# Three more pairs of tiles in reduced-precision parts, and their low parts divided between VectorE and GpSimd

## The chip, the core and the metric

The kernel runs on one core of a Trainium2 chip. The metric is the device time of one execution in microseconds, taken as a median of several executions. The trace of the kernel before is one profiled execution; its times are counted from the start of its span.

## The reference, cut to what matters

For 2048 samples, 39 embedding rows of 16 numbers are looked up. They run through three layers of a compressed interaction network, and a small dense network follows:

```python
x0 = xk = e                                  # [2048, 39, 16]
for idx, (W, b) in enumerate(params):        # three layers, 128 maps each
    z = einsum('bhd,bkd,hks->bsd', x0, xk, W) + b
    z = relu(z)
    # layers 0 and 1: first 64 maps are the next xk, the other 64 go to direct; layer 2: all 128
logit = sum(concat(direct), axis=-1)         # over the 16 numbers: [2048, 256]
h = relu(concat([logit, dense_ctx]) @ W_top1 + b_top1)
h = relu(h @ W_top2 + b_top2);  y = h @ W_top3
```

So each layer multiplies x0 by xk elementwise, for every pair of fields (VectorE), and contracts the products with weights (TensorE). All is float32.

## The kernel before, in words

**Tiling.** The samples are cut into 16 groups of 128, a group into 4 chunks of 32 samples; a chunk has 32 x 16 = 512 columns, 64 chunks in all. The rows (h, k) of a layer are cut into tiles of 128 rows. Layer 0 has 7 tiles of up to 117 rows (symmetric pairs of fields are folded, `x0_diag`), layers 1 and 2 have 20 tiles each, the last of them with only 64 different rows (`x0_pairs`). VectorE makes the products of up to four tiles in one instruction, called a slot here: 2 slots for layer 0, 5 for layer 1, 5 for layer 2. The products go to `prod`, a ring of four slots; a slot is given back when TensorE has finished with it (`slot_free`), so VectorE is at most four slots ahead.

**Plain and split tiles.** A plain tile is one float32 matmul, which the trace shows as two records of TensorE (L686). A split tile is three matmuls (L709) in the type float32r: ScalarE rounds the product to a high part (`pair_hi`, L526), another engine subtracts that from the product and writes the low part (`pair_lo`, `low_part`, L210), and TensorE multiplies high by low weights, low by high weights, and high by high weights. Two tiles are split together, a pair. Before, 11 pairs are split per chunk: 5 in layer 1, 5 in layer 2, 1 in layer 0. The tile of 64 rows is also split, with two matmuls (the half tile, `half_parts`, L522 and L206). The list `SPLITS` gives, for each layer, slot, first tile in the slot and number of tiles. `pair_hi` and `pair_lo` hold two pairs each, so ScalarE may round a pair only when TensorE has finished the pair two before it.

**Who does what.** VectorE makes all products (L412), the low parts of layers 0 and 1, and the sums over the 16 numbers (`sum01` L442, `sum2` L449). GpSimd makes the low parts of layer 2 and, behind them in each chunk, issues that chunk's share of the indirect DMAs that gather the embedding rows of a later group (L345, 39 per group). ScalarE rounds (L526, L522), and applies bias and relu: `hand_on` (L535, L536) makes the next layer's xk in two halves, L562 and L616 make the `direct` parts, L569 does layer 2. It copies x0 to `xk0` in PSUM for the products of layer 0 (L559).

**Order.** Each engine has a written order inside a loop over the groups. TensorE runs, per chunk, layer 1, then layer 0 of the next chunk, then layer 2; in the second chunk of a group it also transposes the next group's embeddings, between layers 1 and 0. VectorE makes the products in the same order, each low part one product behind the product it belongs to. ScalarE runs roundings in order of use; those of layer 2 are interrupted after the fourth entry of its list (`EARLY`) by `hand_on(0, ...)` and `direct_0()`. Products of layer 2 need `xk2`, which needs all of layer 1 from TensorE; products of layer 1 need `xk1` from layer 0, which was made a phase earlier. SyncE and the queue of ScalarE load `x0_pairs` (two buffers) and `x0_diag` for the next chunk.

**End.** After the last chunk the dense network runs on TensorE from `logit01` and `logit2`, which hold the sums of all samples in SBUF (L768).

## Time and profile before

| | us |
|---|---|
| median of 3 executions | 2551.4 (2550.67 to 2551.43) |
| the profiled execution | 2557.0 |
| its span, first to last instruction | 2555.3 |
| TensorE busy with matmuls | 2434.8 |
| VectorE busy | 2269.2 |
| GpSimd busy | 1558.9 |
| ScalarE busy | 1175.5 |

The mean granted TensorE clock is 0.995 of full speed. Matmuls are pipelined and their ends are modelled, so the distance from one start to the next tells what one costs, not the duration of a record. A duration of VectorE, ScalarE or GpSimd is that of the instruction; two instructions behind each other on VectorE overlap by about 0.08 us.

### The profile page before, as it was taken

Reading aid. Unit: us, or ns where it says so; the run is one execution under the profiler, and the core shown is the slowest. Engines: PE = TensorE matmul, PEld = TensorE weight load, DVE = VectorE, ACT = ScalarE, POOL = GpSimd, SP = SyncE. Lnnn points to the kernel's source line nnn. Section 1 sums busy time; section 2 is a strip of 40 time slices with the busy share of each in tenths; the row PEclk is TensorE's granted clock in tenths of the full one; section 3 lists DMA queues with packets and bytes.
Section 4 is the critical chain, followed back from the end, with each engine's and each line's share of the span. In section 5 each row is a group of like instructions: output and inputs, shape, how many; then the busy total and the mean of one; then the engine's idle time right before and its main releaser. Section 6 shows DMA issues by size and latency. Waiting matters only on the chain.

```text
span 2555.3 us, 25999 instructions
## 1 busy us (share of the span) xinstructions
PE 2434.8 (95%) x7712; PEld 1425.0 (56%) x7712; DVE 2269.2 (89%) x1356; ACT 1175.5 (46%) x1414; POOL 1558.9 (61%) x1030
## 2 busy tenths in 40 slices
PE   0499999999999999999999999999999999999999
PEld 0255555555555555555555565555555555555553
DVE  0499999999999999999999999999999999999960
ACT  0145444444444454544444444544444444445442
POOL 6466676666667666766666676667666666743240
PEclk9899999999999999999999999999999999999999
DMA  2977776877678687767867776777778677776610
GB/s 60 231 189 195 204 211 173 218 199 195 183 209 218 179 203 201 210 175 208 212 190 188 215 214 177 199 208 208 175 216 205 186 193 211 209 176 201 195 30 0
DMA packets 262599, 477.02 MB, mean 187 GB/s; under 512 B 19371, under 2 KB 37675, under 8 KB 262501
## 3 DMA queue, kind: packets, MB, share of 16 engines
q1 hardware_dynamic: 141622, 271.05, 39.4%
q10 hardware_dynamic: 100480, 200.29, 28.8%
q0 software_dynamic: 20480, 5.47, 1.4%
q8 instruction: 9, 0.15, 0.0%
q14 instruction: 8, 0.07, 0.0%
HBM read 468.99 MB, written 7.74 MB: 187 GB/s over the span
## 4 chain that ended last, share of the span: by engine, by line
PE 69%; POOL 11%; DVE 6%; issue 5%; DMA 5%; ACT 2%; another core or an unknown queue 1%; SPq 0%; POOLq 0%; DVEq 0%; ACTq 0%
PE z L686 35%; PE z L709 31%; POOL emb L345 6%; DVE prod L412 4%; POOL pair_lo L210 4%; DMA emb<-in_tbl,idx 4%; PE xk L768 1%; PE z L768 1%; ACT pair_hi L526 1%; POOL half_parts L206 1%; DVE logit L442 1%; DVE pair_lo L210 1%; PE turned L667 1%; DMA x_diag<-x_transposed 1%
## 5 line engine op out<-in xcount | busy, mean ns | idle before, releaser
L412 DVE TENSOR_TENSOR prod<-x_pairs,xk 128x2048 f32<-128x2048 f32 x640 | 1436.7, 2284 | 74.7 <-PE z L709 49.6
L686 PE MATMUL z<-prod,w_plain 128*128 128x512 f32 (+2 forms) x2944 | 1383.3, 594 | 41.8 <-issue 26.4
L526 ACT CAST pair_hi<-prod 128x1024 fp32r<-128x1024 f32 x703 | 735.6, 1046 | 1077.5 <-PE z L709 756.0
L210 POOL TENSOR_TENSOR pair_lo<-prod,pair_hi 128x1024 fp32r<-128x1024 f32 x320 | 764.0, 2387 | 641.9 <-ACT pair_hi L526 625.2
L686 PEld LDWEIGHTS z<-prod,w_plain 128*128 128x128 f32 (+2 forms) x2944 | 555.7, 189 | 475.5 <-issue 400.7
L345 POOL DMA_INDIRECT emb<-in_tbl,idx x624 | 701.5, 1124 | 189.4 <-issue 173.2
L709 PE MATMUL z<-pair_hi,w_lo 128*128 128x512 f32 (+1 forms) x1408 | 787.6, 559 | 2.3 <-DVE pair_lo L210 1.7
L709 PE MATMUL z<-pair_hi,w_hi 128*128 128x512 f32 (+1 forms) x1408 | 556.3, 395 | 0.0
L709 PE MATMUL z<-pair_lo,w_hi 128*128 128x512 f32 (+1 forms) x1408 | 555.5, 395 | 0.0
L210 DVE TENSOR_TENSOR pair_lo<-prod,pair_hi 128x1024 fp32r<-128x1024 f32 (+1 forms) x384 | 468.5, 1220 | 49.4 <-ACT pair_hi L526 49.4
L709 PEld LDWEIGHTS z<-pair_hi,w_lo 128*128 128x128 f32 (+1 forms) x1408 | 265.5, 189 | 297.3 <-POOL pair_lo L210 137.1
L709 PEld LDWEIGHTS z<-pair_lo,w_hi 128*128 128x128 f32 (+1 forms) x1408 | 266.3, 189 | 154.7 <-issue 122.9
L412 DVE TENSOR_TENSOR prod<-x_diag,xk 117x2048 f32<-117x2048 f32 (+1 forms) x128 | 257.7, 2014 | 71.4 <-ACT xk L559 71.4
L709 PEld LDWEIGHTS z<-pair_hi,w_hi 128*128 128x128 f32 (+1 forms) x1408 | 264.7, 188 | 65.0
L535 ACT ACTIVATE xk<-z,columns 64x512 f32<-64x512 f32 x128 | 83.0, 648 | 148.6 <-PE z L709 132.1
L206 POOL TENSOR_TENSOR half_parts<-prod,half_parts 64x512 fp32r<-64x512 f32 x64 | 83.2, 1300 | 5.5
L667 PE MATMUL turned<-ident,emb 128*78 128x128 f32 x128 | 18.3, 288 | 69.9 <-DMA emb<-in_tbl,idx 69.9
L536 ACT ACTIVATE xk<-z,columns 64x512 f32<-64x512 f32 x128 | 83.5, 652 | 1.6
L522 ACT CAST half_parts<-prod 128x512 fp32r<-128x512 f32 x128 | 78.7, 615 | 0.0
L442 DVE TENSOR_REDUCE logit<-direct 128x512 f32 (+1 forms) x64 | 67.9, 1060 | 0.0
L335 POOL DMA_DIRECT2D idx<-in_ids x16 | 9.5, 597 | 82.9 <-DMA emb<-in_tbl,idx 82.6
L667 PEld LDWEIGHTS turned<-ident,emb 128*78 128x78 f32 x128 | 14.3, 149 | 76.5 <-issue 76.3
(50 smaller groups left out, 566.2 us busy)
## 6 DMA issues: line engine op xcount, KB each, us to landing
x_pairs<-x_transposed ACTq DMA_DIRECT2D x64, 2432.0 KB
x_pairs<-x_transposed SPq DMA_DIRECT2D x64, 2432.0 KB
x_diag<-x_transposed SPq DMA_DIRECT2D x128, 546.0 KB
x_diag<-x_transposed ACTq DMA_DIRECT2D x64, 546.0 KB
x_pairs<-x_transposed SPq DMA_DIRECT2D x64, 256.0 KB
emb<-in_tbl,idx POOLq DMA_INDIRECT x624
x_diag<-x_transposed SPq DMA_DIRECT2D x128, 78.0 KB
x_transposed<-stage SPq DMA_DIRECT2D x32, 156.0 KB
```

Of the source, the lines that this page charges most:

```text
L206: engine.tensor_tensor(half_parts[HALF:P], held[HALF:P, at, :], half_parts[HALF:P].bitcast(F32), ALU.subtract).then_inc(lo_ready[layer], 1)
L210: engine.tensor_tensor(pair_lo[0:rows, pair % PAIR_RING], held[0:rows, at:at + 2, :], pair_hi[0:rows, pair % PAIR_RING].bitcast(F32), ALU. ...
L345: nc.gpsimd.indirect_dma_start(out=emb[:, f * D:(f + 1) * D], out_offset=None, in_=tables[f], in_offset=bass.IndirectOffsetOnAxis(ap=idx[: ...
L412: nc.vector.tensor_tensor(prod[0:rows, pos % RING, 0:n, :], a, xk.unsqueeze(1).broadcast_to([rows, n, N]), ALU.mult).then_inc(prod_ready, 1)
L442: nc.vector.tensor_reduce(logit01[:, bass.ds(chunk * CB, CB)], direct01[:].rearrange("p (d b) -> p b d", b=CB), AXIS.X, ALU.add).then_inc( ...
L522: nc.scalar.copy(half_parts[:], held[:, at, :]).then_inc(hi_ready, 1)
L526: nc.scalar.copy(pair_hi[0:rows, pair % PAIR_RING], held[:, at:at + 2, :]).then_inc(hi_ready, 1)
L535: nc.scalar.activation(xk[0:HALF], z[layer][0:HALF], ACT.Relu, bias=b[0:HALF])
L536: nc.scalar.activation(xk[HALF:P], z[layer][0:HALF], ACT.Relu, bias=b[0:HALF]).then_inc(xk_ready[layer], 1)
L667: ins = nc.tensor.transpose(turned[d // 4][0:2 * F, d % 4 * P:(d % 4 + 1) * P], emb[:, d:F * D:D // 2], ident[:])
L686: ins = nc.tensor.matmul(z[n][:], w, held[0:rows, i, :], start=(k == 0 and i == plain[0]), stop=(k == last_slot and not here and i == plai ...
L709: ins = nc.tensor.matmul(z[n][:], w, x, start=False, stop=(k == last_slot and s is here[-1] and i == len(terms) - 1))
```

## The change

- `SPLITS` gets three more pairs per chunk: tiles 2 and 3 of slot 1 in layer 1, tiles 2 and 3 of slot 3 in layer 2, and all four tiles of the first slot of layer 0 in place of two. A fourth field says who makes the low part. Layer 0's four tiles are rounded by one instruction and subtracted by one.
- Low parts: in layer 1 VectorE makes three pairs and GpSimd three pairs and the half tile; in layer 2 GpSimd makes five pairs, VectorE one pair and the half tile; layer 0 stays with VectorE.
- The buffers of parts hold six tiles (`hi_parts`, `lo_parts`, `PLACES`), so three pairs in place of two.
- GpSimd issues gathers between the low parts of layer 1 (one, one, one and five), and the rest at the end of the chunk; its wait for the gathers at each chunk's start is gone, except once in a group.
- TensorE waits for both slots of layer 0 at once and takes the plain tiles first (`layer0`). The transposes stand before layer 1 of the second chunk.
- VectorE's products of layer 0 read x0 from SBUF (`x0_diag[:, T0, :]`), and the copy to PSUM (`copy_xk0`) is gone. `direct01` lies in that PSUM bank in place of SBUF.
- The sums of a group are kept in a window of 128 columns, and SyncE stores it to DRAM once per group (`store_window`, two DMAs); at the end they are loaded again with the dense network's weights.

Core of the diff:

```diff
@@ -52,25 +52,45 @@
 L0_FIRST = range(0, T0, QUAD)
 FIRST_TILE = (0, 4, 16, 8, 12)
-SPLITS = {0: [(0, 0, 2)],
-          1: [(0, 0, 2), (1, 0, 2), (2, 0, 2), (2, 3, 1), (3, 0, 2), (4, 0, 2)],
-          2: [(0, 0, 2), (1, 0, 2), (2, 0, 2), (2, 3, 1), (3, 0, 2), (4, 0, 2)]}
-EARLY = {1: 4, 2: 4}
+V, G = "VectorE", "GpSimd"
+SPLITS = {0: [(0, 0, 4, V)],
+          1: [(0, 0, 2, V), (1, 0, 2, G), (1, 2, 2, V), (2, 0, 2, V), (2, 3, 1, G), (3, 0, 2, G),
+              (4, 0, 2, G)],
+          2: [(0, 0, 2, G), (1, 0, 2, G), (2, 0, 2, G), (2, 3, 1, V), (3, 0, 2, G), (3, 2, 2, V),
+              (4, 0, 2, G)]}
+EARLY = {1: 5, 2: 4}
 SPLITS_C = sum(len(SPLITS[n]) for n in SPLITS)
-GATHERS_AHEAD = 30
-GATHERS_AT = [range(30, F), range(0, 10), range(10, 20), range(20, 30)]
-PAIR_RING = 2
...
+GATHERS_AHEAD = 31
+GATHERS_AT = [(range(31, F), (1, 1, 1, 5, 0)), (range(0, 10), (1, 1, 1, 5, 2)),
+              (range(10, 20), (1, 1, 1, 5, 2)), (range(20, 31), (1, 1, 1, 5, 3))]
+NO_GATHERS = (range(0), (0, 0, 0, 0, 0))
+assert all(len(fields) == sum(at) for fields, at in GATHERS_AT)
+PARTS = 6
+PLACES, tile = {}, 0
+for n in (1, 0, 2):
+    PLACES[n] = []
+    for _, _, m, _ in SPLITS[n]:
+        PLACES[n].append(tile % PARTS)
+        tile += m if m > 1 else 0
+assert all(place + m <= PARTS for n in SPLITS for (_, _, m, _), place in zip(SPLITS[n], PLACES[n]))
 SPLIT_TILES = {n: [(FIRST_TILE if n else L0_FIRST)[k] + at + i
-                   for k, at, m in SPLITS[n] for i in range(m) if m == 2] for n in SPLITS}
+                   for k, at, m, _ in SPLITS[n] for i in range(m) if m > 1] for n in SPLITS}
 PLAIN_TILES = {n: [t for t in range(TX - 1 if n else T0) if t not in SPLIT_TILES[n]] for n in SPLITS}
 W_ORDER = (1, 2, 0)
 W_SPLITS = {n: len(SPLIT_TILES[n]) + (n > 0) for n in SPLITS}
 X0_DIAG_DMAS, X0_PAIRS_DMAS, ST_DMAS = 2 * DIAG, 3, 4
...
+        def low_part(engine, layer, pos, at, m, place, done):
...
+                                     half_parts[0:HALF].bitcast(F32),
+                                     ALU.subtract).then_inc(done, 1)
             else:
-                engine.tensor_tensor(pair_lo[0:rows, pair % PAIR_RING], held[0:rows, at:at + 2, :],
-                                     pair_hi[0:rows, pair % PAIR_RING].bitcast(F32),
-                                     ALU.subtract).then_inc(lo_ready[layer], 1)
+                engine.tensor_tensor(lo_parts[0:rows, place:place + m, :], held[0:rows, at:at + m, :],
+                                     hi_parts[0:rows, place:place + m, :].bitcast(F32),
+                                     ALU.subtract).then_inc(done, 1)
...
+            def store_window(which, bt):
+                window, stored = ((window01, window01_stored), (window2, window2_stored))[which]
+                cols = sums[which, :, bass.ds(ahead(bt * P), P)]
+                sp.dma_start(cols, window).then_inc(stored, 16)
...
+                    if c == 0:
+                        sp.wait_ge(summed01, bt * CHUNKS + 1)
+                        store_window(0, bt)
+                    if c == 1:
+                        sp.wait_ge(summed2, bt * CHUNKS + 2)
+                        store_window(1, bt)
                     if c == 2 and not last:
...
+            def lows_of(n, chunk, done, split, pos, gathers):
+                for i, (k, at, m, who) in enumerate(SPLITS[n]):
+                    if who == G:
+                        pool.wait_ge(hi_ready, split + i + 1)
+                        if done > 0:
+                            pool.wait_ge(lo_ready[G], chunk * LOWS_C[G] + done)
+                        low_part(nc.gpsimd, n, pos + k, at, m, PLACES[n][i], lo_ready[G])
+                        done += 1
+                        gather(next(gathers, []))
+                return done
             def group(bt, fields_at):
-                pair = PAIRS[0]
-                fields_done = 0 if isinstance(bt, int) and bt == GROUPS - 1 else GATHERS_AHEAD
                 for c in range(CHUNKS):
                     chunk = bt * CHUNKS + c
-                    pool.wait_ge(gathered, 16 * ((bt + 1) * F + fields_done))
-                    fields = fields_at[c]
-                    if fields and fields[0] == 0:
+                    fields, counts = fields_at[c]
+                    ends = [sum(counts[:i + 1]) for i in range(len(counts))]
+                    gathers = iter([fields[end - count:end] for end, count in zip(ends, counts)])
+                    if c == 1 and len(fields):
+                        pool.wait_ge(gathered, 16 * (bt + 2) * F)
                         pool.sem_inc(waits_held, 1)
                         load_indices(bt + 2)
-                    pair, pos = pair + PAIRS[1], SL0 + c * SLC + SLX
-                    split = len(SPLITS[0]) + chunk * SPLITS_C + len(SPLITS[1])
+                        start_group(bt + 2, False)
+                    split, pos = len(SPLITS[0]) + chunk * SPLITS_C, SL0 + c * SLC
+                    done = lows_of(1, chunk, 0, split, pos, gathers)
+                    split, pos = split + len(SPLITS[1]), pos + SLX
                     if not (isinstance(bt, int) and bt == GROUPS - 1 and c == CHUNKS - 1):
-                        pair, pos, split = pair + PAIRS[0], pos + SL0, split + len(SPLITS[0])
-                    for i, (k, at, n) in enumerate(SPLITS[2]):
-                        pool.wait_ge(hi_ready, split + i + 1)
-                        if i > 0:
-                            pool.wait_ge(lo_ready[2], chunk * len(SPLITS[2]) + i)
-                        low_part(nc.gpsimd, 2, pos + k, at, n, pair)
-                        pair += n == 2
-                    if fields and fields[0] == 0:
-                        start_group(bt + 2, False)
-                    gather(fields)
-                    fields_done += len(fields)
+                        split, pos = split + len(SPLITS[0]), pos + SL0
+                    lows_of(2, chunk, done, split, pos, iter([]))
+                    gather(next(gathers))
             load_indices(0)
             start_group(0, True)
...
+            def subtract(late, split):
+                for n, pos, place, k, at, m, who in late:
+                    if who == V:
+                        dve.wait_ge(hi_ready, split + 1)
+                        low_part(nc.vector, n, pos + k, at, m, place, lo_ready[V])
+                    split += 1
+                return split
+            def splits_of(n, pos, slot):
+                return [(n, pos, place, *s) for s, place in zip(SPLITS[n], PLACES[n]) if s[0] == slot]
+            def products(n, copies, xk, slot, pos, late, split):
+                first_tile, rows, tiles = (FIRST_TILE, P, TX) if n else (L0_FIRST, R0, T0)
+                for k, first in enumerate(first_tile):
+                    product(slot + k, pos + k, copies[0:rows, first:min(first + QUAD, tiles), :],
+                            xk[0:rows])
+                    split = subtract(late, split)
+                    late = splits_of(n, pos, k)
+                return late, split
...
@@ -468,22 +521,25 @@
                     dve.wait_ge(x0_pairs_in[c % 2],
                                 16 * X0_PAIRS_DMAS * (bt * (CHUNKS // 2) + c // 2 + 1))
                     dve.wait_ge(xk_ready[0], chunk + 1)
-                    steps = layer(1, copies, xk1, slot, pos)
-                    pair_after = pair + PAIRS[1]
+                    late, split = products(1, copies, xk1, slot, pos, [], split)
+                    slot, pos = slot + SLX, pos + SLX
                     if not (last and c == CHUNKS - 1):
-                        steps += layer(0, x0_diag, xk0, slot + SLX, pos + SLX)
-                        pair_after += PAIRS[0]
-                    products(steps, split, pair, chunk + 1)
-                    slot, pos = slot + len(steps), pos + len(steps)
-                    sum2(chunk)
+                        dve.wait_ge(x0_diag_in, 16 * X0_DIAG_DMAS * (chunk + 2))
+                        late, split = products(0, x0_diag, x0_diag[:, T0, :], slot, pos,
+                                                     late, split)
+                        slot, pos = slot + SL0, pos + SL0
+                    split = subtract(late, split)
+                    sum2(bt, c)
                     dve.wait_ge(xk_ready[1], chunk + 1)
+                    late = []
                     for k in range(SLX):
                         product(slot + k, pos + k, copies[:, FIRST_TILE[k]:FIRST_TILE[k] + QUAD, :],
                                 xk2[:])
                         if k == 1:
-                            sum01(chunk)
-                    pair = pair_after + PAIRS[2]
+                            sum01(bt, c)
+                        split = subtract(late, split)
+                        late = splits_of(2, pos, k)
+                    split = subtract(late, split)
             with dve.Fori(0, GROUPS - 1) as bt:
                 group(bt, False)
...
+            def round_splits(n, some, slot, pos, used_by):
+                rows = P if n else R0
+                for (k, at, m, _), place in list(zip(SPLITS[n], PLACES[n]))[some]:
...
-                        nc.scalar.copy(pair_hi[0:rows, pair % PAIR_RING], held[:, at:at + 2, :]
+                        act.wait_ge(slot_free, RING + used_by[place + m - 1] + 1)
+                        nc.scalar.copy(hi_parts[0:rows, place:place + m, :], held[:, at:at + m, :]
                                        ).then_inc(hi_ready, 1)
-                        held_by.append(slot + k)
-                        pair += 1
...
@@ -604,14 +654,12 @@
                         load_second_half(bt, c + 1)
                     elif not last:
                         load_second_half(bt + 1, 0)
-                    pair = round_splits(SPLITS[1][:EARLY[1]], P, slot, pos, pair, held_by)
+                    round_splits(1, slice(0, EARLY[1]), slot, pos, used_by)
                     direct_2(chunk, slot)
-                    if not (last and c == CHUNKS - 1):
-                        copy_xk0(chunk + 1)
-                    pair = round_splits(SPLITS[1][EARLY[1]:], P, slot, pos, pair, held_by)
+                    round_splits(1, slice(EARLY[1], None), slot, pos, used_by)
                     slot, pos = slot + SLX, pos + SLX
...
@@ -622,14 +670,14 @@
                     if c == 1 and not last:
                         fill_stage(bt + 1)
                     if last and c == CHUNKS - 1:
-                        round_splits(SPLITS[2], P, slot, pos, pair, held_by)
+                        round_splits(2, slice(0, None), slot, pos, used_by)
                     else:
                         slot, pos = slot + SL0, pos + SL0
-                        pair = round_splits(SPLITS[2][:EARLY[2]], P, slot, pos, pair, held_by)
+                        round_splits(2, slice(0, EARLY[2]), slot, pos, used_by)
                         hand_on(0, xk1, b0_sb, slot)
-                        act.wait_ge(summed01, chunk + 1)
+                        act.wait_ge(summed01, chunk + 2)
                         direct_0()
-                        pair = round_splits(SPLITS[2][EARLY[2]:], P, slot, pos, pair, held_by)
+                        round_splits(2, slice(EARLY[2], None), slot, pos, used_by)
             with act.Fori(0, GROUPS - 1) as bt:
                 group(bt, False)
...
+            def layer0(slot, pos, lows):
+                pe.wait_ge(prod_ready, slot + SL0)
+                held = prod[:, (pos + SL0 - 1) % RING]
+                t = L0_FIRST[SL0 - 1]
+                for i in range(T0 - t):
+                    plain_part(0, t, i, held, i == 0, False)
+                s, = SPLITS[0]
+                split_part(0, 0, s, PLACES[0][0], lows, False, True).then_inc(slot_free, SL0)
+                lows[s[3]] = lows[s[3]] + 1
             pe.wait_ge(ident_ready, 1)
             transpose_group(0)
             pe.wait_ge(w0_summed, 2)
...
                     slot, pos = SL0 + chunk * SLC, SL0 + c * SLC
-                    pe.wait_ge(direct01_ready, 2 * chunk + 1)
-                    pair = layer(1, slot, pos, chunk * len(SPLITS[1]), pair)
-                    slot, pos = slot + SLX, pos + SLX
+                    lows = {V: len(SPLITS[0]) + chunk * LOWS_C[V], G: chunk * LOWS_C[G]}
                     if c == 1 and not last:
                         transpose_group(bt + 1)
+                    pe.wait_ge(direct01_ready, 2 * chunk + 1)
+                    layer(1, slot, pos, lows)
+                    slot, pos = slot + SLX, pos + SLX
                     if not (last and c == CHUNKS - 1):
-                        pair = layer(0, slot, pos, (chunk + 1) * len(SPLITS[0]), pair)
+                        layer0(slot, pos, lows)
                         slot, pos = slot + SL0, pos + SL0
                     pe.wait_ge(summed2, chunk + 2)
-                    pair = layer(2, slot, pos, chunk * len(SPLITS[2]), pair)
+                    layer(2, slot, pos, lows)
             with pe.Fori(0, GROUPS - 1) as bt:
                 group(bt, False)
```

## Rows read from the trace of the kernel before

**Rows 1.** The page's first part: busy us, share of the span, instructions.

```profile
PE 2434.8 (95%) x7712; PEld 1425.0 (56%) x7712; DVE 2269.2 (89%) x1356; ACT 1175.5 (46%) x1414; POOL 1558.9 (61%) x1030
```

**Rows 2.** Waits: engine, line, releaser: us, times, longest us.

```profile
ACT pair_hi L526 <- PE z L709: 756.0, 438, 5.2
...
PEld z L709 <- POOL pair_lo L210: 137.1, 189, 1.3
```

**Rows 3.** Timeline, TensorE, layer 1: start us, us, engine, line, operation, count.

```profile
1298.64 1.88 PE L686 MATMUL z<-prod,w_plain 128*128 128x512 f32 x4
...
1300.59 0.39 PE L709 MATMUL z<-pair_lo,w_hi 128*128 128x512 f32 x1
...
1301.52 0.39 PE L709 MATMUL z<-pair_hi,w_hi 128*128 128x512 f32 x1
...
1301.75 1.88 PE L686 MATMUL z<-prod,w_plain 128*128 128x512 f32 x4
```

**Rows 4.** Timeline, ScalarE: end of layer 1 in the first and in the last chunk.

```profile
129.05 0.65 ACT L535 ACTIVATE xk<-z,columns 64x512 f32<-64x512 f32 x1 [2.07 <-PE z L709]
...
2459.71 0.65 ACT L535 ACTIVATE xk<-z,columns 64x512 f32<-64x512 f32 x1 [5.13 <-PE z L709]
```

**Rows 5.** Timeline, ScalarE, one chunk from the end of its layer 1.

```profile
1277.34 0.65 ACT L535 ACTIVATE xk<-z,columns 64x512 f32<-64x512 f32 x1 [2.01 <-PE z L709]
...
1281.09 1.05 ACT L526 CAST pair_hi<-prod 128x1024 fp32r<-128x1024 f32 x1 [1.73 <-DVE prod L412]
...
1288.12 0.65 ACT L535 ACTIVATE xk<-z,columns 64x512 f32<-64x512 f32 x1
...
1290.17 1.05 ACT L526 CAST pair_hi<-prod 128x1024 fp32r<-128x1024 f32 x1
...
1292.36 1.04 ACT L526 CAST pair_hi<-prod 128x1024 fp32r<-128x1024 f32 x1 [1.13 <-PE z L709]
...
1314.01 0.65 ACT L535 ACTIVATE xk<-z,columns 64x512 f32<-64x512 f32 x1 [2.01 <-PE z L709]
```

**Rows 6.** Timeline, TensorE, the same chunk: layer 0, two pairs of layer 2.

```profile
1277.14 1.88 PE L686 MATMUL z<-prod,w_plain 117*128 117x512 f32 x4
...
1284.64 0.50 PE L709 MATMUL z<-pair_hi,w_lo 128*128 128x512 f32 x1
...
1294.02 0.50 PE L709 MATMUL z<-pair_hi,w_lo 128*128 128x512 f32 x1
```

**Rows 7.** Timeline, GpSimd, the same chunk: lows, then gathers.

```profile
1282.22 4.85 POOL L210 TENSOR_TENSOR pair_lo<-prod,pair_hi 128x1024 fp32r<-128x1024 f32 x2 [8.18 <-ACT pair_hi L526]
...
1296.59 0.95 POOL L345 DMA_INDIRECT emb<-in_tbl,idx  x1
...
1299.10 0.94 POOL L345 DMA_INDIRECT emb<-in_tbl,idx  x1 [0.30 <-issue]
...
1300.35 1.60 POOL L345 DMA_INDIRECT emb<-in_tbl,idx  x1 [0.30 <-issue]
```

**Rows 8.** Timeline, VectorE, the same chunk.

```profile
1278.02 0.69 DVE L449 TENSOR_REDUCE logit<-z 128x512 f32 x1
...
1278.77 4.49 DVE L412 TENSOR_TENSOR prod<-x_pairs,xk 128x2048 f32<-128x2048 f32 x2
...
1283.17 1.05 DVE L442 TENSOR_REDUCE logit<-direct 128x512 f32 x1
...
1299.91 1.23 DVE L210 TENSOR_TENSOR pair_lo<-prod,pair_hi 128x1024 fp32r<-128x1024 f32 x1 [0.77 <-ACT pair_hi L526]
```

**Rows 9.** Groups by shape: operands, count, busy us, mean ns, idle before.

```profile
L412 DVE TENSOR_TENSOR prod<-x_diag,xk 117x2048 f32<-117x2048 f32 x64 | 145.9, 2280 | 71.4 <-ACT xk L559 71.4
...
L412 DVE TENSOR_TENSOR prod<-x_diag,xk 117x1536 f32<-117x1536 f32 x64 | 111.8, 1747 | 0.0
...
L576 ACT CAST w_hi<-x_pairs 128x1408 fp32r<-128x1408 f32 x2 | 2.6, 1363 | 7.9 <-DMA x_pairs<-in_w 7.9
```

**Rows 10.** Timeline, TensorE, first matmuls of the last layer 2.

```profile
2463.49 3.75 PE L686 MATMUL z<-prod,w_plain 128*128 128x512 f32 x4 [3.82 <-DVE prod L412]
```

193 lines of the change are left out of this document (92 added, 101 removed).

## Prediction

> **What bounds the kernel now.** I read the busy times first: TensorE is busy 95% of the span, VectorE 89% [rows 1]. Then the waits: what ScalarE waits for is TensorE giving buffers back (756 us in all), and the only standing wait of TensorE's weight loads for another engine's work is 137 us for low parts from GpSimd [rows 2]. So it is TensorE's order of work, with small stalls. The timeline gives the prices. Five split matmuls start 0.93 us from first to last, so one costs 0.2325 us. A slot with two plain and two split tiles takes 3.11 us (1298.64 to 1301.75), which leaves (3.11 - 6 x 0.2325)/4 = 0.429 per plain record [rows 3]. A plain tile (two records) costs 0.858, a split one 0.698.
>
> Per chunk before: layers 1 and 2 have four slots of 3.11 and one of 2.72 (one plain tile, a pair and the half tile), 15.16 each; layer 0 has 10 plain records and 6 split matmuls, 5.69. Together 36.01. An ordinary chunk really takes 1314.01 - 1277.34 = 36.67 [rows 5], so 0.66 is lost in waits. Over all, 63 chunks take 2330.66 us, 36.99 each [rows 4]; the 0.32 above 36.67 is the transposes, 1.3 us per group.
>
> **The change, part by part.**
>
> *Matmuls.* Six more tiles are split: 6 x 0.16 = 0.97 less per chunk, 61 us in all. Layer 0 takes 6 x 0.429 + 12 x 0.2325 = 5.36. A slot of two pairs (slot 1 of layer 1, slot 3 of layer 2) takes 2.79 and has no plain tile in front. Layers 1 and 2: 3 x 3.11 + 2.72 + 2.79 = 14.84. Together 35.04. What decides is whether the low parts come that early. I walk one chunk; T is the moment TensorE leaves layer 1 (1277.14 [rows 6]).
>
> *First pair of layer 2.* Before: the first product starts at T+1.63 [rows 8], because xk2 comes from the end of layer 1; the rounding at T+3.95 [rows 5], GpSimd's low at T+5.08, 2.4 long [rows 7], the matmul at T+7.50 [rows 6]. TensorE would have been ready at 5.69 + 1.72 = T+7.41. This chain is thus already as long as TensorE's work beside it. Afterwards TensorE is ready at 5.36 + 1.72 = 7.08, the chain is unchanged: 0.4 wait, and the gain in layer 0 is given back.
>
> *Fourth pair of layer 2.* ScalarE rounds the third pair when the third product ends (T+9.1), then the half tile, and then does `hand_on(0)` and `direct_0`, which take 1290.17 - 1288.12 = 2.05 [rows 5]. The rounding of pair (3,0) starts at about T+12.8, ends 13.85, GpSimd's low ends 16.3. TensorE is there at 8.90 + 3.11 + 2.72 = T+14.73, and the slot has no plain tile to cover. Before, the same matmul started at T+16.88 [rows 6] behind 1.72 of plain work. Wait: 1.6. Layer 2 ends at T+22.25.
>
> *Second slot of layer 1.* Pair (1,0) uses the parts that the last pair of layer 2 gives back, so it is rounded 0.20 after layer 2 ends (the gap of row 1292.36 [rows 5] to the slot's end, 1292.16), ends at +1.25, GpSimd's low at +3.7; the slot is due at +3.11: wait 0.65. VectorE's low of (1,2) is in time.
>
> *Layer 0's four tiles.* Their places include those of pair (3,0) of layer 1, so they are rounded only 2.9 before the end of layer 1. For 2048 columns no row exists: 1.36 is the rounding of 1408 [rows 9], twice that bounds it above; the slope from 1.05 (1024) to 1.36 gives 1.89, taken. VectorE's low of 2048: between 1.23 [rows 8] and twice that, I take 2.28, the product of the same size [rows 9]. It ends at T+1.3, the sum follows (0.75 [rows 8]), and layer 2's first product starts at T+1.98 in place of 1.63: 0.35.
>
> Without any other effect: 35.04 + 0.4 + 1.6 + 0.65 + 0.35 = 38.0 per chunk, 1.4 above 36.67.
>
> *GpSimd.* Per chunk eight pairs (2.45 apart), a half tile (1.30, estimate: about half a pair) and 9.75 gathers (1.25 apart [rows 7]) make 33 us, near the whole chunk. A gather that starts (1300.35) while VectorE subtracts two SBUF operands (1299.91 to 1301.14) takes 1.60 in place of 0.94 [rows 7, 8]: it is held until the subtraction ends. VectorE has eight instructions with two SBUF operands per chunk: six lows, and now both products of layer 0 (2.28 and 1.75 [rows 9]; before, their xk came from PSUM). Low (1,0) ends at T+26.0 (22.25 + 3.7). Behind it GpSimd does a gather (1.25), the half tile (1.3), a gather held by VectorE's low of (2,0) (1.25 + 0.45), low (3,0) (2.45), a gather held by layer 0's first product (1.25 + 0.8) and low (4,0) (2.45): 11.2, so T+37.2. Layer 1 began at 22.25, and its last pair's matmul is due at 22.25 + 0.65 + 3.11 + 2.79 + 2.72 + 3.11 + 1.72 = 36.35: wait 0.8. The five gathers behind it, the first held by the low of layer 0, end at the next T+6.8, where the first low of layer 2 wanted to start at 5.08: wait 2.1 in place of the 0.4; it absorbs all but 0.1 of the fourth pair's 1.6 and the 0.35. Sum: 35.04 + 2.1 + 0.1 + 0.65 + 0.8 = 38.7.
>
> *At no cost.* `sum01` from PSUM: 0.69 (`sum2`) to 1.05 (now) [rows 8]; taken as 0.7, at most 0.36 on ScalarE's chain. `copy_xk0` gone: ScalarE has idle time (46% busy). Windows: each store waits for a sum already made and is needed 35 us later; behind it on SP stand the chunk loads, whose own waits come later. Bounds: 0 to one landing (about 2 us) per group, 30 us. Transposes before layer 1: they cost 1.7 there but cover the 0.65, about the 1.3 of before. Start and end: the weights are the same bytes; four more loads at the end run beside the last chunk, 0 to 3 us.
>
> **Sum.** 38.7 - 36.67 = 2.0 per chunk, x 63 = 126 us. Profiled execution: 2557.0 + 126 = 2683; the median of runs lies 5.6 below it, 2551.4 + 126 = 2677.
>
> **Rivals.**
>
> 1. *TensorE stays the bound* (faster). The chains run further ahead with three pairs of buffers, and waits stay 0.66: 35.70 per chunk, 0.97 x 63 = 61 less, 2490. For it: three pairs in place of two release much of ScalarE's 756 us. Against it: the chains above hang on xk2 and on ScalarE's order, not on buffers. It decides if the low of (3,0) ends before T+14.7.
> 2. *Products of layer 0 hold GpSimd's lows.* If a GpSimd low waits for a two-operand instruction of VectorE as the gather did, low (4,0) also waits for layer 0's second product, about 1.4 more: 40.1, +214, 2766.
> 3. *Each holds the other.* If also VectorE waits while GpSimd subtracts, VectorE's low (2,0) comes 1.2 late (half tile on GpSimd), layer 0's products start behind low (3,0) and then hold low (4,0), whose matmul waits 3.2 in place of 0.8. 38.7 + 1.2 + 2.4 = 42.3: 5.6 x 63 = 353, 2904. No low of GpSimd meets such an instruction in the rows before: GpSimd's stand beside products with a PSUM operand, VectorE's beside gathers. A wait of 3.8 us was followed by matmuls at half pace (3.75 for four records [rows 10] against 1.88 [rows 3]), so long waits may cost more.
> 4. *Waits and gain cancel* (1.63 of waits per chunk), no change.
>
> The Trainium skill (SBUF — State Buffer, Who interferes with whom) says that a VectorE instruction with two SBUF inputs and a GpSimd instruction that reads SBUF exclude each other, and whichever starts first keeps the port to its end. By that rule the third rival holds, 2904; the held gather agrees with half of it, VectorE held by GpSimd is in no row.
>
> **Chances.** Forecast (own range 2625 to 2710) 0.42; rival 1 0.20; rival 2 0.12; rival 3 0.20; rival 4 0.06. The forecast's mechanism can be halved in size without changing sign. The range goes from 2490, which takes half of rival 1, to 2900, half of rival 3; what is outside is 0.2. A change of 0.2% is about what these executions can tell from none. Faster 0.20, same 0.05 (rival 4, mostly), slower 0.75.
>
> **What would show it.** Right: the distance between ends of layer 1 at 38 to 39; gaps on TensorE in front of the first pair of layer 2, of pair (3,0) there and of (1,0) in layer 1, ended by GpSimd; five gathers between low (4,0) and the first low of layer 2; TensorE's busy share near 90%. Rival 1: no such gap above 0.2. Rivals 2 and 3: lows of GpSimd longer than 2.4, and for 3 also subtractions of VectorE above 1.22. Wrong altogether if the distance is under 36.7.

## The result and the profile after

The changed kernel takes 2844.2 us (median of four, 2842.7 to 2846.5), the kernel before 2551.4 us beside it (2550.7 to 2552.1): 1.115 times as long [1.114, 1.117]. The forecast was 2677, at most 2900. The sign came, and the size was 293 us in place of 126.

First part of the page after, its chain of waits, and the longest waits (us, times, longest us):

```profile
span 2842.3 us, 27866 instructions
...
PE 2468.4 (87%) x8096; PEld 1517.3 (53%) x8096; DVE 2583.0 (91%) x1294; ACT 1317.9 (46%) x1478; POOL 2287.6 (80%) x1222
...
DVE 45%; POOL 20%; issue 15%; PE 13%; ACT 4%; DMA 1%; DVEq 1%; ACTq 0%; SPq 0%; POOLq 0%
```

```profile
ACT hi_parts L583 <- DVE prod L462: 859.6, 449, 5.8
PEld z L745 <- POOL lo_parts L235: 418.9, 360, 3.1
...
ACT hi_parts L583 <- PE z L745: 264.7, 197, 2.4
...
PE z L745 <- POOL lo_parts L235: 238.3, 202, 2.3
```

Against [rows 1], TensorE's share fell from 95 to 87%. VectorE has 62 instructions fewer and yet 314 us more of busy time, GpSimd 729 us more (192 lows more are 459 of it at 2.39). Against [rows 2], ScalarE waits less for TensorE (265 in place of 756) and most for VectorE's products (860), and TensorE waits three times as long for GpSimd's lows. VectorE stands for 45% of the chain.

Where in the span? The ends of layer 1 of the first and the last chunk (timeline of ScalarE) answer to [rows 4]:

```profile
125.28 0.65 ACT L590 ACTIVATE xk<-z,columns 64x512 f32<-64x512 f32 x1 [3.82 <-PE z L745]
...
2747.45 0.65 ACT L590 ACTIVATE xk<-z,columns 64x512 f32<-64x512 f32 x1 [5.17 <-PE z L745]
```

63 chunks take 2622.2, that is 41.62 each in place of 36.99: 4.63 x 63 = 292 us, all of it. The four chunks of a group are alike (41.6 to 41.7 each). The last seven of the 63 differ: no gather is issued any more there, and they take 39.7 each, the 56 before them 41.9.

The groups by shape, mean ns of one second from the right, answer to [rows 7 to 9]:

```profile
L235 POOL TENSOR_TENSOR lo_parts<-prod,hi_parts 128x1024 fp32r<-128x1024 f32 x512 | 1283.9, 2508 | 303.3 <-ACT hi_parts L583 285.7
L388 POOL DMA_INDIRECT emb<-in_tbl,idx x624 | 911.1, 1460 | 158.5 <-issue 125.1 <-ACT hi_parts L583 12.6 <-DMA idx<-in_ids 9.1
...
L235 DVE TENSOR_TENSOR lo_parts<-prod,hi_parts 128x1024 fp32r<-128x1024 f32 x256 | 434.0, 1695 | 19.8 <-ACT hi_parts L583 19.8
...
L235 DVE TENSOR_TENSOR lo_parts<-prod,hi_parts 117x2048 fp32r<-117x2048 f32 x64 | 242.7, 3793 | 21.4 <-ACT hi_parts L583 21.1 <-ACT hi_parts L639 0.3
L462 DVE TENSOR_TENSOR prod<-x_diag 117x2048 f32<-117x2048 f32 x64 | 203.9, 3185 | 68.3 <-DMA x_diag<-x_transposed 68.3
...
L462 DVE TENSOR_TENSOR prod<-x_diag 117x1536 f32<-117x1536 f32 x64 | 124.8, 1950 | 0.0
...
L230 DVE TENSOR_TENSOR half_parts<-prod,half_parts 64x512 fp32r<-64x512 f32 x64 | 110.4, 1726 | 0.0
```

On the mean, every kind of VectorE instruction with two operands in SBUF is longer than the same work takes undisturbed: a low of two tiles 1.70 us for 1.22, the half tile 1.73 for 0.69, layer 0's first product 3.19 for 2.28. The products with an operand in PSUM stayed at 2.28. A record holds the time for which an instruction stood started and held.

The place that costs most, the end of layer 1, in the timeline of one chunk (GpSimd, VectorE, and TensorE's waiting matmul):

```profile
1455.56 2.39 POOL L235 TENSOR_TENSOR lo_parts<-prod,hi_parts 128x1024 fp32r<-128x1024 f32 x1
...
1456.83 4.95 DVE L462 TENSOR_TENSOR prod<-x_diag 117x2048 f32<-117x2048 f32 x2
...
1458.11 2.82 POOL L388 DMA_INDIRECT emb<-in_tbl,idx  x1 [0.16 <-ACT hi_parts L583]
...
1460.22 1.90 ACT L583 CAST hi_parts<-prod 117x2048 fp32r<-117x2048 f32 x1 [2.23 <-DVE prod L462]
...
1460.95 3.03 POOL L235 TENSOR_TENSOR lo_parts<-prod,hi_parts 128x1024 fp32r<-128x1024 f32 x1
1462.15 3.98 DVE L235 TENSOR_TENSOR lo_parts<-prod,hi_parts 117x2048 fp32r<-117x2048 f32 x1 [0.37 <-ACT hi_parts L583]
...
1464.03 0.50 PE L745 MATMUL z<-hi_parts,w_lo 128*128 128x512 f32 x1 [2.29 <-POOL lo_parts L235]
1464.13 2.82 POOL L388 DMA_INDIRECT emb<-in_tbl,idx  x1 [0.15 <-issue]
```

GpSimd's low of pair (3,0) runs to 1457.95, and layer 0's first product, started at 1456.83, is done only at 1460.2 (ScalarE rounds it then): 1.1 held plus 2.28. The gather started beside it ends 0.7 after it, at 1460.93. By then the second product runs; the low of pair (4,0) starts and takes 3.03, 0.64 more than 2.39. Layer 0's low stands behind that one: 3.98 in place of 2.28. Four links, each held by the one before, and TensorE stood 2.29 us.

To see which wait a run moves, I took TensorE's waits by place: the distance between starts at each slot, less 0.429 per plain record and 0.2325 per split matmul, mean over ordinary chunks (not the first of a group). "Period" is the distance between ends of layer 1 in such chunks; in the kernel before, the second of a group is left out in place of the first, because its transposes stand there. The period without waits is 35.05 for the 14 pairs of the change, 36.0 before and 35.7 in e15; with the waits, each row adds up within 0.15. L2, L1, L0 are the layers; a blank is a place without a wait to speak of.

| kernel | L0 | L2 first pair | L2 (3,0) | L1 (1,0) | L1 (2,0) | L1 (4,0) | other | period |
|---|---|---|---|---|---|---|---|---|
| before | | 0.21 | 0.26 | | | | 0.17 | 36.7 |
| after | 0.41 | 0.91 | 0.74 | 0.80 | 0.75 | 2.39 | 0.56 | 41.7 |
| e1 | | 0.77 | 1.32 | 0.77 | | | | 38.0 |
| e2 | | 1.22 | 0.82 | 0.81 | 0.75 | 0.05 | | 38.8 |
| e3 | 0.10 | 0.39 | 1.29 | 0.77 | | 2.35 | 0.84 | 40.9 |
| e4 | | 0.77 | 0.28 | 0.88 | | | | 37.1 |
| e5 | | 1.22 | 1.24 | 0.80 | 0.75 | 0.06 | | 39.2 |
| e7 | 0.14 | 1.27 | 0.52 | 0.81 | 0.75 | 2.40 | 0.46 | 41.5 |
| e11 | | 1.50 | 1.32 | 0.77 | 0.75 | 0.25 | 0.22 | 40.0 |
| e13 | | 3.19 | 0.25 | 0.85 | 0.75 | 0.86 | 1.21 | 42.2 |
| e14 | | 1.23 | 0.53 | 0.81 | 0.75 | 0.05 | | 38.5 |
| e15 | | 0.83 | 0.27 | | | | 0.07 | 36.9 |

One thing is mixed into these means. In the changed kernel TensorE was granted the lower level of its clock, 1.2 in place of 2.4 GHz, in 32 stretches, 116 us in all. Thirty of them are 3.4 us long and begin 0.1 to 1.5 us after TensorE has started again behind the wait at L1 (4,0). The 12 of its first 56 periods that touch none take 41.7, with waits of 1.86 at the first pair of layer 2, 0.51 at (3,0), 0.8 at L1 (1,0), 0.76 at (2,0) and 2.57 at (4,0). The other 44 take 41.9: matmuls at half pace lengthen layer 0, and the wait at the first pair of layer 2 is shorter by as much (0.2 beside 1.5 us in layer 0 in several periods). So the clock is worth about 0.2 per period, some 10 us in all, but it moves waits from one column to another.

### The profile page after: what moved, and what is told of

Read it like the earlier page. It is cut to its first block, busy times and chain, and to the rows that moved or that the text cites. A ratio compares the mean times of both kernels' runs of the same rounds, so it can differ in the third digit from the quotient of the medians.

```text
span 2842.3 us, 27866 instructions
## 1 busy us (share of the span) xinstructions
PE 2468.4 (87%) x8096; PEld 1517.3 (53%) x8096; DVE 2583.0 (91%) x1294; ACT 1317.9 (46%) x1478; POOL 2287.6 (80%) x1222
## 4 chain that ended last, share of the span: by engine, by line
DVE 45%; POOL 20%; issue 15%; PE 13%; ACT 4%; DMA 1%; DVEq 1%; ACTq 0%; SPq 0%; POOLq 0%
DVE prod L462 31%; POOL emb L388 12%; DVE lo_parts L235 10%; POOL lo_parts L235 8%; PE z L745 7%; PE z L724 4%; ACT hi_parts L583 3%; DVE half_parts L230 3%; DMA x_pairs<-x_transposed 1%; PE z L833 1%; PE xk L833 1%; PE direct L833 0%; ACT xk L591 0%; DVEq L461 0%; DVEq L470 0%
## 5 line engine op out<-in xcount | busy, mean ns | idle before, releaser
L235 POOL TENSOR_TENSOR lo_parts<-prod,hi_parts 128x1024 fp32r<-128x1024 f32 x512 | 1283.9, 2508 | 303.3 <-ACT hi_parts L583 285.7
L583 ACT CAST hi_parts<-prod 128x1024 fp32r<-128x1024 f32 x831 | 914.9, 1112 | 1131.0 <-DVE prod L462 859.6
L745 PE MATMUL z<-hi_parts,w_lo 128*128 128x512 f32 (+1 forms) x1792 | 893.2, 498 | 269.9 <-POOL lo_parts L235 238.3
L745 PE MATMUL z<-hi_parts,w_hi 128*128 128x512 f32 (+1 forms) x1792 | 721.3, 403 | 0.0
L745 PE MATMUL z<-lo_parts,w_hi 128*128 128x512 f32 (+1 forms) x1792 | 714.9, 399 | 0.0
L235 DVE TENSOR_TENSOR lo_parts<-prod,hi_parts 128x1024 fp32r<-128x1024 f32 (+1 forms) x320 | 676.7, 2115 | 41.2 <-ACT hi_parts L583 40.9
L745 PEld LDWEIGHTS z<-hi_parts,w_lo 128*128 128x128 f32 (+1 forms) x1792 | 339.5, 189 | 626.3 <-POOL lo_parts L235 418.9
L745 PEld LDWEIGHTS z<-lo_parts,w_hi 128*128 128x128 f32 (+1 forms) x1792 | 342.8, 191 | 137.3 <-issue 85.6
L462 DVE TENSOR_TENSOR prod<-x_diag 117x2048 f32<-117x2048 f32 (+1 forms) x128 | 323.7, 2568 | 68.3 <-DMA x_diag<-x_transposed 68.3
L745 PEld LDWEIGHTS z<-hi_parts,w_hi 128*128 128x128 f32 (+1 forms) x1792 | 340.3, 190 | 79.9
```

The lines of the kernel that those rows point to most:

```text
L235: engine.tensor_tensor(lo_parts[0:rows, place:place + m, :], held[0:rows, at:at + m, :], hi_parts[0:rows, place:place + m, :].bitcast(F32) ...
L462: nc.vector.tensor_tensor(prod[0:rows, pos % RING, 0:n, :], a, xk.unsqueeze(1).broadcast_to([rows, n, N]), ALU.mult).then_inc(prod_ready, 1)
L583: nc.scalar.copy(hi_parts[0:rows, place:place + m, :], held[:, at:at + m, :]).then_inc(hi_ready, 1)
L745: ins = nc.tensor.matmul(z[n][:], w, x, start=(first and i == 0), stop=(last and i == len(terms) - 1))
```

## Experiments

Theory A: VectorE's instructions with two SBUF operands and GpSimd's lows hold each other. Theory B: it is the order on ScalarE and GpSimd, with the gathers held as before, and no more. Theory C: VectorE is simply the bound.

### Which operands: e1, e2, e3

e2 gives only layer 0's products a PSUM operand, e3 only VectorE's lows, e1 both.

```
-    late, split = products(0, x0_diag, x0_diag[:, T0, :], slot, pos,
+    late, split = products(0, x0_diag, xk1[:], slot, pos,          # e1, e2 (op min)
-    hi_parts[0:rows, place:place + m, :].bitcast(F32),
+    bank[0:rows].unsqueeze(1).broadcast_to([rows, m, N]),          # e1, e3, VectorE only
```

The bank holds other numbers than the operand that it stands for, and in layer 0 a minimum stands for the multiplication or the subtraction; the same is so in e4 and e8, which build on e1. e5 below does the whole computation.

> The changed kernel with one difference: on VectorE every instruction that read two SBUF operands (the low parts, and the products of layer 0) reads its second operand from a PSUM bank that holds a finished xk, with the same shape; the arithmetic of those instructions is thereby another. Theory A (VectorE and GpSimd exclude each other while one has two SBUF operands and the other reads SBUF): VectorE's low of 1024 columns falls from 1.70 to 1.22 us, the half tile from 1.73 to 0.69, layer 0's low from 3.79 to 2.28, GpSimd's low from 2.51 to 2.39, a gather from 1.46 to 0.95; a chunk falls from 41.6 to 38.0 us (the hand walk without any hold), 2844 - 227 = 2617 us. Theory B (the chains of waits and ScalarE's order alone): the durations fall but the chunk stays above 40.5, over 2780 us. Theory C (VectorE is simply the bound): the chunk falls by VectorE's full 5.5 us to 36.1, about 2500 us.

> The changed kernel, only layer 0's products read their second operand from PSUM (another arithmetic there). Theory A: the two products fall from 3.19 and 1.95 us to 2.28 and 1.75, and GpSimd's last low of layer 1 is no longer held: 1.1 to 2.3 us per chunk less, 2700 to 2775 us. Theory B: at most 0.5 us per chunk, over 2810.

> The changed kernel, only VectorE's low parts read their second operand from PSUM (another arithmetic there). Theory A: their mean durations fall by 0.48 (pairs), 1.04 (half tile) and 1.5 us (layer 0), 4.4 us per chunk in all, of which the hand walk leaves 1.7 to 2.5 on the path: 2687 to 2740 us. Theory B: under 0.5 us per chunk, over 2810.

Measured: e1 2671.6 (1.048 [1.046, 1.050]), e2 2666.9 (1.046 [1.044, 1.048]), e3 2838.9 (1.114 [1.112, 1.116]). Groups by shape of e2:

```profile
L235 POOL TENSOR_TENSOR lo_parts<-prod,hi_parts 128x1024 fp32r<-128x1024 f32 x512 | 1229.3, 2401 | 321.0 <-ACT hi_parts L586 305.5
...
L462 DVE TENSOR_TENSOR prod<-x_diag,xk 117x2048 f32<-117x2048 f32 x63 | 143.3, 2274 | 0.0
L462 DVE TENSOR_TENSOR prod<-x_diag,xk 117x1536 f32<-117x1536 f32 x63 | 109.7, 1742 | 0.0
```

The same place in e2, a timeline:

```profile
1397.62 3.94 DVE L462 TENSOR_TENSOR prod<-x_diag,xk 117x2048 f32<-117x2048 f32 x2
1398.89 0.95 POOL L388 DMA_INDIRECT emb<-in_tbl,idx  x1 [0.16 <-ACT hi_parts L586]
1399.87 2.39 POOL L235 TENSOR_TENSOR lo_parts<-prod,hi_parts 128x1024 fp32r<-128x1024 f32 x1
```

Beside the same two products with one operand in PSUM the gather takes 0.95 and the low 2.39: no link of the chain is left, and the wait at (4,0) fell from 2.39 to 0.05. So A holds for layer 0's products, and two instructions per chunk cost 177 us, more than A's 70 to 145. C is out: e1 stays at 38.0 per chunk, not 36.1. The lows' share was the surprise, for e3 lies where B had put it (over 2810): with their operand moved alone (e3) 5 us are gained, and moved on top of the products (e1 against e2) 5 are lost. In e2 TensorE waits 0.75 at (2,0), because VectorE's low before it, that of (1,2), is held by GpSimd's low of (1,0) (2.14 in place of 1.22, from 1389.85); e1 has that wait no more, and has more at (3,0) and on the index load (below). In ordinary chunks e1 is at 38.0, what the prediction's walk without any hold gave.

### The whole computation with that operand in PSUM: e5

xk0 gets its PSUM bank and its copy on ScalarE back, and direct01 moves to SBUF.

```
-        direct01 = ps("direct01")
+        xk0 = ps("xk0")
+    nc.scalar.copy(xk0[0:R0], x0_diag[0:R0, T0, :]).then_inc(xk0_ready, 1)
```

> The changed kernel with one part undone, all arithmetic as in the reference: ScalarE copies x0 to a PSUM bank again for layer 0's products, and direct01 lies in SBUF again. If the 177 us that the first products' second operand cost are the port and not the other numbers in that bank, this lands near the 2667 of that run: 2665 to 2695 us (sum01 0.37 us longer, one copy of 0.58 on ScalarE). If they came from the changed numbers or another side effect: 2800 or more.

Measured 2693.8 (1.057 [1.055, 1.059]), in the range. It is 27 above e2, all of it at L2 (3,0), which waits 1.24 for 0.82. The timeline of e5 shows where that comes from:

```profile
1425.02 1.06 DVE L496 TENSOR_REDUCE logit<-direct 128x32 f32<-128x512 f32 x1
...
1425.21 1.04 ACT L585 CAST hi_parts<-prod 128x1024 fp32r<-128x1024 f32 x1 [1.19 <-DVE prod L464]
1428.31 1.05 ACT L585 CAST hi_parts<-prod 128x1024 fp32r<-128x1024 f32 x1 [2.05 <-DVE prod L464]
```

`sum01` reads SBUF again and takes 1.06 in place of 0.69, so the third product of layer 2 and its rounding come later: 3.10 behind the second rounding, 2.72 in e2 (1410.17 to 1412.89). The copy (0.58) stands in time in which ScalarE waited in e2.

### The same operand in the kernel before: e9

> The kernel before with one part of the change: layer 0's products read x0 from SBUF (x0_diag) in place of PSUM; the copy to PSUM is still made. No low of GpSimd runs in that phase, so VectorE's durations stay (2.28, 1.75, 1.22). But VectorE then has five instructions with two SBUF operands behind each other (low, product, low, product, low, 8 us), and in the run with lows by layer one gather was held for 9.6 us by such a string. If a string holds GpSimd as a whole, one gather per chunk takes 8 to 9.6 us and the first low of layer 2 comes up to 1.5 us late: 2551 to 2645 us, I expect 2590. If GpSimd gets in between two instructions, nothing changes: 2551.

```
-    steps += layer(0, x0_diag, xk0, slot + SLX, pos + SLX)
+    steps += layer(0, x0_diag, x0_diag[:, T0, :], slot + SLX, pos + SLX)
```

Measured 2548.8 (0.9995 [0.9986, 1.0004]): nothing, where 2590 was expected. The groups show why: GpSimd's low keeps 2.388 and the products 2.284 and 1.753; only the gathers rose, from 1.12 to 1.19. Before, GpSimd has no low beside layer 0's products, so two SBUF operands there are free. They cost in the company that the divided lows bring. This also excludes that the products are slower by themselves with two SBUF operands.

### The gathers: e11, e13

e11 leaves out all gathers and index loads of the loop; e13 moves a gather from between lows (3,0) and (4,0) to behind (4,0).

```
-GATHERS_AT = [(range(31, F), (1, 1, 1, 5, 0)), (range(0, 10), (1, 1, 1, 5, 2)),
+GATHERS_AT = [(range(31, F), (1, 1, 0, 6, 0)), (range(0, 10), (1, 1, 0, 6, 2)),
```

> The changed kernel without the gathers and index loads inside the loop over the groups (each group reuses the rows of the second; that part is left out): GpSimd has 12 us per chunk less to do. If the 2.4 us in front of the last pair of layer 1 come from layer 0's two products, which start when that pair's rounding does and run without a gap, they stay, and only part of the 0.9 at the first pair of layer 2 goes: 0.4 us per chunk less, 2800 to 2830 us. If GpSimd's load is the cause (the way of the prediction: gathers in front of lows), 1.7 to 3 us per chunk less: 2655 to 2735.

> The changed kernel with one gather moved: none between lows (3,0) and (4,0) of layer 1, six behind (4,0) (counts 1, 1, 0, 6). Theory D (a chain of two holds: the gather behind (3,0) is held by layer 0's first product, so GpSimd asks for (4,0) only when the second product has begun): low (4,0) gets in between the two products, TensorE's 2.4 us in front of it fall to about 0.3, VectorE's second product takes 3.9 in place of 1.95, and some of it comes back at the first pair of layer 2: 1.2 us per chunk less, 2770 us (2750 to 2800). Theory E (GpSimd has too much to do, wherever a gather stands): no change, 2830 or more.

e11 took 2748.4 (1.077 [1.076, 1.079]), e13 2958.1 (1.161 [1.160, 1.163]). Timeline of e13:

```profile
946.12 2.41 POOL L235 TENSOR_TENSOR lo_parts<-prod,hi_parts 128x1024 fp32r<-128x1024 f32 x1
...
947.41 7.12 DVE L462 TENSOR_TENSOR prod<-x_diag 117x2048 f32<-117x2048 f32 x2
...
948.72 4.19 POOL L235 TENSOR_TENSOR lo_parts<-prod,hi_parts 128x1024 fp32r<-128x1024 f32 x1 [0.19 <-ACT hi_parts L583]
...
954.44 2.28 DVE L235 TENSOR_TENSOR lo_parts<-prod,hi_parts 117x2048 fp32r<-117x2048 f32 x1
```

Without the gather, low (4,0) already stands when the first product ends and goes between the two; now the second product waits (3.80 mean for 1.75). In both runs (4,0) waits less: 0.86 in e13 and 0.25 in e11, for 2.39. For e11 I had expected that wait to stay; its second product takes 3.89, as in e13. That confirms the order of the chain. But in e13 six gathers now stand ahead of layer 2's first low, whose wait goes from 0.91 to 3.19: what was gained in layer 1 (1.5) was lost there and in the slots behind it, and each group's first period rose to 46.0. So the time lies where theory E had put it (2830 or more), though the link that D names came out. Part of it is the clock: of the ordinary periods, the 28 that touch a stretch at the lower level take 42.9, the 14 others 41.5. e11's 96 us are what gathers cost with the holds in place, between the two cases that I had written down. The changed kernel's own last seven periods, which have no gathers, say the same: 39.7 each, with at most 0.2 at (4,0), and e11 has 40.0.

### ScalarE's order and the index load: e4, e7, e8, e14

`EARLY = {1: 5, 2: 6}` rounds L2's pair (3,0) before `hand_on(0)`: e4 is e1 with it, e7 the changed kernel with it. e8 (from e4) and e14 (from e5) also issue the next index load behind the third low of layer 2 in the first chunk of a group, one chunk earlier than the code that waits for it.

```
-EARLY = {1: 5, 2: 4}
+EARLY = {1: 5, 2: 6}
+                        if then and i == 2:
+                            then()        # next_indices, e8 and e14
```

> As the first of these, and ScalarE rounds pairs (3,0) and (3,2) of layer 2 before hand_on(0) and direct_0 (EARLY 6 in place of 4). If the wait for pair (3,0) comes from ScalarE's order, as the prediction said (1.6 us, with GpSimd's low ending at T+16.3), it falls to about 0.3: 1.3 us per chunk less than the first, about 2535 us if that is 2617. If that wait is covered by something else, the two are equal.

> The changed kernel, only ScalarE's order: pairs (3,0) and (3,2) of layer 2 rounded before hand_on(0) (EARLY 6 in place of 4). It was worth 37 us where no instruction of VectorE was held. Here VectorE never idles between products, so a wait of TensorE in layer 2 hands nothing on: under 0.3 us per chunk, 2825 to 2844 us. If TensorE's waits add up whatever the cause (the prediction's way), 0.4 to 0.6 per chunk less: 2805 to 2820.

> As the run with one SBUF operand and EARLY 6 (2635 us), and GpSimd issues the load of the next group's indices behind its third low of layer 2 in a group's first chunk, in place of at the start of the second; its wait stands before the first gather. In that run the load was issued behind 2.4 MB of x0_pairs and took 7.4 us, with GpSimd and then TensorE waiting, and every fourth chunk took 41.9 in place of 37.1 us. If that is the cause: 4.8 x 15 = 72 us less, 2563. If the transposes in that chunk are: no change, 2635.

> The mixed division with layer 0's operand in PSUM (2694 us), EARLY 6 and the early load of the indices; the slots of layer 1 as in the changed kernel. The order was worth 0.9 us per chunk where nothing was held: 2637 us if it adds up. The kernel with layer 1 reordered as well took 2637.5, so equality says that the reordering brought nothing (its waits of 0.8 and 0.75 went to the first pair of layer 2); if waits add up it is slower, 2690.

Measured: e4 2634.8 (1.033), e7 2879.1 (1.130 [1.128, 1.132]), e8 2597.3 (1.019 [1.017, 1.021]), e14 2695.2 (1.056 [1.055, 1.058]). L2 (3,0) fell from 1.32 to 0.28 in e4 as said. e7 fell by 0.2 in ordinary chunks and lost 2.7 in each group's first period (44.4 against 41.6). e1 shows how, in its timeline:

```profile
923.54 0.62 SPq L251 DMA_DIRECT2D x_pairs<-x_transposed  x1
923.68 0.63 ACTq L251 DMA_DIRECT2D x_pairs<-x_transposed  x1
924.18 0.60 POOL L379 DMA_DIRECT2D idx<-in_ids  x1
...
932.13 2.35 POOL L235 TENSOR_TENSOR lo_parts<-prod,hi_parts 128x1024 fp32r<-128x1024 f32 x1 [7.35 <-DMA idx<-in_ids]
...
934.53 0.50 PE L752 MATMUL z<-hi_parts,w_lo 128*128 128x512 f32 x1 [2.66 <-POOL lo_parts L235]
```

GpSimd waits 7.35 us for the small index load, issued 0.64 after two of 2.4 MB, and its low stands behind the wait. In the changed kernel the index load goes out 0.01 ahead of them, and GpSimd's next low starts 3.5 later, with ScalarE its last releaser: the load was no longer in question. So a faster GpSimd sequence fell behind the big loads and paid for it (e1: 41.54 in the first period, 38.0 in the others). In e8 that period fell from 41.91 to 39.68, half of what I expected. e14 did not gain: ordinary chunks went from 39.2 to 38.5 and each group's first rose from 39.3 to 41.75. The timeline of e14 shows what takes those 2.5 us:

```profile
1388.12 0.94 POOL L390 DMA_INDIRECT emb<-in_tbl,idx  x1 [0.30 <-issue]
1389.09 7.32 POOL L237 TENSOR_TENSOR lo_parts<-prod,hi_parts 128x1024 fp32r<-128x1024 f32 x3
1398.97 0.60 POOL L380 DMA_DIRECT2D idx<-in_ids  x1 [2.56 <-DMA emb<-in_tbl,idx]
1399.59 5.37 POOL L237 TENSOR_TENSOR lo_parts<-prod,hi_parts 128x1024 fp32r<-128x1024 f32 x2
```

The index load may go out only when the last gather has landed. At its new place GpSimd waits 2.56 us for that and issues for 0.60, and the low of (3,0) stands behind both: TensorE waits 3.09 there in that period, 0.55 in the others. In e8 it is 2.4 for 0.3, which is most of the missing half.

### Dividing the lows otherwise: e6, e10, e12, e15

e6 and e10 give all lows of layer 1 to VectorE and all of layer 2 to GpSimd, with the gathers behind them; e10 also has xk0 in PSUM. e12 is e14 with another order and mixture in layer 1. e15 has the ten pairs of layers 1 and 2 that were there before, layer 0's group of four tiles (twelve pairs in all), and lows by layer. In e10 and e15 a group's first chunk has no gathers and the other three have 13 each.

```
-          1: [(0, 0, 2, V), (1, 0, 2, G), (1, 2, 2, V), (2, 0, 2, V), (2, 3, 1, G), (3, 0, 2, G),
+          1: [(0, 0, 2, V), (1, 0, 2, V), (1, 2, 2, V), (2, 0, 2, V), (2, 3, 1, V), ...   # e6, e10
+          1: [(0, 0, 2, V), (1, 0, 2, G), (2, 0, 2, V), (2, 3, 1, V), (3, 0, 2, G),
+              (3, 2, 2, V), (4, 0, 2, G)],                                                # e12
+          1: [(0, 0, 2, V), (1, 0, 2, V), (2, 0, 2, V), (2, 3, 1, V), (3, 0, 2, V), (4, 0, 2, V)],  # e15
```

> The changed kernel with the low parts divided by layer as before: VectorE makes all of layer 1 (six pairs and the half tile) and layer 0, GpSimd all of layer 2 (six pairs and the half tile), and the gathers stand behind GpSimd's lows. Layer 0's products still read two SBUF operands. Theory A: no low of GpSimd meets a two-operand instruction, so the durations return to 2.28, 1.22 and 2.39; VectorE has 37.1 us of work per chunk and layer 2 waits for GpSimd's 16 us of lows: 38.7 per chunk, 2660 us (2630 to 2700). Theory C (the mix of engines is harmless and layer 0's operand alone costs): VectorE has a pair more to do and it is slower than now, over 2844.

> Lows divided by layer again, with what spoiled that comparison removed: layer 0's operand in PSUM, and no gather in a group's first chunk (13 in each of the others, 39 ahead), so that the transposes before layer 1 do not wait. Arithmetic as in the reference. Theory A: nothing is held; left are the waits of layer 2 for GpSimd's 16 us of lows (1.7 and 1.1 us in the fourth slot) and about 1 in layer 1: 39.3 us per chunk, 2698 us. It then does not beat the mixed division with the same operand in PSUM (2694): the mix of lows costs nothing by itself. If the mix costs, this is 2640 or less.

> Fourteen pairs with every wait found so far attacked, arithmetic as in the reference: layer 0's operand in PSUM, EARLY 6 in layer 2, indices loaded early, in layer 1 the slot with two pairs is the fourth (so pair (1,0) has plain tiles in front), and VectorE makes the half tile's low there. From 39.2 us per chunk of the run with xk0 in PSUM: 0.9 for the order in layer 2, 0.8 for pair (1,0), 0.4 for the held low: 37.1, and 2.4 more in every fourth chunk: 2575 to 2610 us. It would be at best near the kernel before, because the first pair of layer 2 still waits.

> Twelve pairs: only layer 0's two more tiles are split, lows divided by layer as before, five pairs each in layers 1 and 2, layer 0's operand in PSUM, three pairs of buffers, no gather in a group's first chunk; arithmetic as in the reference. TensorE's work falls by 0.33 us per chunk. If, as the prediction says, the first pair of layer 2 hangs on a chain from xk2 that is as long as TensorE's work beside it, the 0.33 come back there and VectorE's 1.06 us more add to them: 36.7 to 37.2 us per chunk, 2551 to 2580. If the gain in layer 0 is real: 36.35, 2531 us.

Measured: e6 3009.7 (1.181 [1.179, 1.183]), e10 2813.4 (1.103 [1.101, 1.105]), e12 2637.5 (1.034 [1.032, 1.035]), e15 2560.7 (1.0044 [1.0030, 1.0058]). e6 failed by something else: the transposes of a group stood before layer 1 and waited for its gathers (first period 54.9, the others 40.6), so its time says nothing on the mixture. Its other periods do: 40.6 against 41.7 after, and VectorE's lows are back at 1.22 and 2.28, GpSimd's at 2.38, as theory A said. e10 is at 41.1 per chunk against 39.2 of e5, with 1.97 and 1.07 in front of the pairs of layer 2's fourth slot; its four periods are alike, so the moved gathers do not matter. Dividing the lows inside a layer (and the gathers with them) thus costs 1.1 per chunk while layer 0's products have two SBUF operands, and gains 1.9 when one is in PSUM. By itself it isn't what made the kernel slow. e12 is the fastest that does the whole computation with 14 pairs, 37.6 in ordinary chunks, and still 0.9 above the kernel before. It is 58 us faster than e14, so its order in layer 1 did bring something: the second of the two cases written down for e14 (2690) came. What is left is mainly 1.44 at the first pair of layer 2, and the index load.

e15 is the cleanest test of "the gain in layer 0 is given back": its period without waits is 35.7 against 36.0, and the first pair of layer 2 waits 0.83 in place of 0.21. No version with more split pairs beat the kernel before.

## Why the prediction was right in sign and short in size

*Matmuls.* 35.04 without waits. The table's waits added to it give the periods (after: 35.04 + 6.56 = 41.6), so the saving of 0.97 per chunk is there, and 5.9 of waits more.

*First pair of layer 2.* 0.4 from latency alone, 2.1 with the gathers in front. Measured 0.77 without holds (e1), 1.22 with gathers held by lows (e2). After, the mean is 0.91, but 1.86 in the periods without a stretch at the lower clock, so the size was nearly right there, partly by luck: the 0.8 at L1 (4,0), on which it stood, came as 2.57, and as 0.05 in e2.

*Fourth pair of layer 2.* 1.6 from ScalarE's order, unless absorbed. e1 shows 1.32, and rounding it earlier (e4) takes 1.04 off. "Absorbed to 0.1" was wrong: 0.74 stayed (0.51 in the periods without the lower clock).

*Second slot of layer 1.* 0.65; 0.77 to 0.88 everywhere.

*Layer 0's four tiles.* The rounding took 1.90 (1.89 estimated), the low 2.28 undisturbed (e3), `sum01` 0.68.

*The step that failed.* "Low (2,0)" and "low (4,0)" were walked with only gathers held by VectorE. I knew from [rows 7, 8] that a gather waits for a two-operand subtraction, and gave the case in which lows and products also hold each other 0.20, the case with nothing beyond the gathers 0.42. The runs decided for the former. Its terms: 1.2 for (2,0), measured 0.75 (after and e2; 0 in e1 and e3, where the low's second operand is in PSUM); 3.2 at (4,0), measured 2.39 (2.57 in the periods without the lower clock); 42.3 per chunk, measured 41.6; 2904 us, measured 2844. The 0.75 has another source than the rival named, GpSimd's half tile. In the changed kernel:

```profile
1447.89 2.40 POOL L235 TENSOR_TENSOR lo_parts<-prod,hi_parts 128x1024 fp32r<-128x1024 f32 x1
...
1449.09 2.29 DVE L235 TENSOR_TENSOR lo_parts<-prod,hi_parts 128x1024 fp32r<-128x1024 f32 x1
...
1453.50 1.21 DVE L235 TENSOR_TENSOR lo_parts<-prod,hi_parts 128x1024 fp32r<-128x1024 f32 x1
```

VectorE's low of (1,2) is held by GpSimd's low of (1,0) and takes 2.29; the low of (2,0), two instructions later, is undisturbed (1.21) and comes late for that reason. Row by row nothing had spoken for the weaker case; that before no low met such an instruction was absence of evidence, and I read it as a reason to leave the effect out.

The Trainium skill (SBUF — State Buffer, Who interferes with whom) says that a VectorE instruction with two SBUF inputs and a GpSimd instruction that reads SBUF exclude each other in both directions. The trace agrees: product 1 held by a low (1456.83), a low held by product 2 (1460.95, 3.03 us), both gone in e2.

*That 2677 is near e2 and e5 (2667, 2694) is partly chance.* Their waits are 1.22, 0.82, 0.81, 0.75, 0.05 where the forecast had 2.1, 0.1, 0.65, 0 and 0.8.

*At no cost.* Start and end: the first end of layer 1 came 3.8 us earlier (in e9, which left that part nearly as it was, it came 4.3 earlier, so this says little), and from the last one to the end of the span it is 94.9 us after and 95.6 before: nothing lost. What I had not priced was the index load. In the changed kernel it is hidden; as soon as the holds go (e1) it costs 3.5 us per group, 56 in all.

*Rivals 1 and 4* are excluded: even without holds, with ScalarE's order mended and the index load moved (e8), the waits are 2.0 per chunk, and the time 2597. Rival 2 (one-sided) is excluded by the product of 3.19 us, which GpSimd held.

## What to carry to other kernels

Before giving one engine work that runs beside another's, list for both which instructions have two operands in SBUF and which pairs will then overlap; the same two products cost nothing (e9) or 177 us (e2) depending on their neighbours. A hold seen once on a light instruction (a gather, 0.66 us) is a reason to price it on all heavier ones. When a chain of holds is broken, look at once at what its delay had kept in order: here a small load that slid behind two large ones.

## What the runs showed of the hardware

A gather can be held for much longer than one instruction: 42 of e6's 624 gathers took over 9 us. In its timeline:

```profile
1005.73 9.59 POOL L388 DMA_INDIRECT emb<-in_tbl,idx  x1 [0.30 <-issue]
1006.07 1.21 DVE L235 TENSOR_TENSOR lo_parts<-prod,hi_parts 128x1024 fp32r<-128x1024 f32 x1
1007.21 2.28 DVE L462 TENSOR_TENSOR prod<-x_diag 117x2048 f32<-117x2048 f32 x1
1009.41 1.22 DVE L235 TENSOR_TENSOR lo_parts<-prod,hi_parts 128x1024 fp32r<-128x1024 f32 x1
1010.54 1.75 DVE L462 TENSOR_TENSOR prod<-x_diag 117x1536 f32<-117x1536 f32 x1
1012.21 2.28 DVE L235 TENSOR_TENSOR lo_parts<-prod,hi_parts 117x2048 fp32r<-117x2048 f32 x1
```

Five such instructions of VectorE stand back to back, none of them longer than usual, and the gather, which started 0.34 ahead of the first of them, ends 0.83 after the last. It held none of them; a low of GpSimd in its place would have (e13). In e9 a gather did end between two such instructions, so whether it always loses is open.

The same product took as long with its second operand in SBUF as in PSUM (2.284 and 2.280), so moving it costs nothing where nobody is beside it; a reduction took 0.68 from PSUM (`sum01`) against 1.05 from SBUF before [rows 8].

The mean granted clock of TensorE was 0.995 of 2.4 GHz before, 0.980 after, 0.962 in e13 and 0.997 in e2. In the changed kernel 30 of the 32 stretches at the lower level, of the kind seen in [rows 10], began right behind the longest wait (2.4 us), at L1 (4,0), and the periods that such stretches touch are 0.2 us longer on the mean (41.9 against 41.7). In e13 it is more (42.9 against 41.5).
